# Rounding of packed counts in two instructions, and visit tables in uint16, in a four-layer graph network

## The reference, cut to what matters

```python
h = relu(layernorm(x)); x = x + GIN(h, src, dst)           # segment sum of h[src] by dst, two linear layers
h = relu(layernorm(x)); x = x + Attention(h, edges, ...)   # segment softmax by target, then a linear layer
h = relu(layernorm(x)); x = x + SAGE(h, src, dst)          # mean of h[src] by dst, two linear layers
h = relu(layernorm(x)); x = x + Weighted(h, src, dst, w)   # segment sum of w * h[src], one linear layer
```

## Time and profile before

| | |
|---|---|
| median of 3 runs | 5038.48 us (5023.93, 5038.48, 5147.51) |
| span of the profiled execution | 5145.3 us |
| DVE busy | 3822.7 us (74%) |
| PE busy | 3841.6 us (75%) |
| count layer of layer 0, first to last rounding (L1360) | 1380.7 to 1778.5 us |
| count layer of layer 2, first to last rounding (L1360) | 4184.5 to 4585.7 us |
| granted TensorE clock, mean | 0.909 |

### The profile page before, as it was taken

One profiled execution on the slowest core, in us unless ns is written; L12 is line 12 of the kernel. 1 busy time (PEld: TensorE's weight loads), 2 busy tenths in 40 slices (PEclk: granted clock), 3 DMA queues, 4 the chain that ended last, 5 costly groups with the idle time before them and its releaser, 6 DMA issues. The chain is left out here.

```text
span 5145.3 us, 93266 instructions
## 1 busy us (share of the span) xinstructions
PE 3841.6 (75%) x26234; PEld 2720.9 (53%) x26235; DVE 3822.7 (74%) x6359; ACT 1550.3 (30%) x3023; POOL 2737.6 (53%) x2300
## 2 busy tenths in 40 slices
PE   4685555550199968888888888888886348889999
PEld 2443222220189835555555555555554248888888
DVE  3516999991299989999999999999996699970000
ACT  2372234560101130122333444445552430020000
POOL 3430199996732227777777777777776232210000
PEclk8799999995599989999999999999997569999999
DMA  9674423346155444454555666666665535568887
GB/s 168 175 234 111 97 100 126 159 175 198 66 193 209 163 140 106 120 146 142 157 165 169 184 184 188 193 196 197 205 204 159 186 113 200 200 213 300 298 297 254
DMA packets 594376, 912.02 MB, mean 177 GB/s; under 512 B 107452, under 2 KB 519442, under 8 KB 575022
## 3 DMA queue, kind: packets, MB, share of 16 engines
q1 hardware_dynamic: 413024, 521.23, 31.2%
q10 hardware_dynamic: 117359, 250.68, 13.4%
q0 software_dynamic: 63872, 138.75, 11.3%
HBM read 608.33 MB, written 311.94 MB: 179 GB/s over the span
## 5 line engine op out<-in xcount | busy, mean ns | idle before, releaser
L1964 POOL DMA_INDIRECT at_qg<-q_d,at_slot x1616 | 1601.2, 991 | 495.8 <-issue 492.2
L986 PE MATMUL bw_ps<-bw_mov,bw_sta 128*128 128x392 bf16 x7056 | 1590.0, 349 | 19.2 <-issue 7.2
L986 PEld LDWEIGHTS bw_ps<-bw_mov,bw_sta 128*128 128x128 bf16 x7056 | 640.4, 102 | 365.0 <-issue 95.6
L2007 PE MATMUL at_psk<-at_kp,at_hot 128*128 x4848 | 611.7, 234 | 286.8 <-DVE at_qg L2085 244.4
L1051 POOL DMA_INDIRECT tv_rows<-ed_d,tv_place x101 | 628.2, 6219 | 339.1 <-DMA edv_d<-tv_rows 211.0
L2007 PEld LDWEIGHTS at_psk<-at_kp,at_hot 128*128 128x128 bf16 x4848 | 439.1, 101 | 624.1 <-issue 418.1
L889 PE MATMUL ba_ps<-ba_mov,ba_sta 128*128 128x392 bf16 x1968 | 380.4, 338 | 352.6 <-DVE ba_sta L830 309.1
L874 DVE TENSOR_SCALAR ba_mov<-iota,key,scale 128x392 bf16<-128x392 f16 x1968 | 592.4, 365 | 2.8 <-PEq L853 2.8
L970 DVE TENSOR_TENSOR bw_sta<-bw_raw,kw 128x1024 bf16<-128x1024 bf16 x882 | 561.2, 689 | 0.0
L830 DVE TENSOR_TENSOR bw_mov<-bw_ps,lo 128x3136 bf16<-128x3136 f16 x294 | 523.4, 1780 | 7.6 <-PE bw_ps L986 5.4
L1566 PE MATMUL at_p3t<-tile,room 128*128 128x256 f32 (+1 forms) x2450 | 524.2, 376 | 4.6 <-ACT room L1150 4.6
(11 more groups left out here) (537 smaller groups left out, 4668.3 us busy)
## 6 DMA issues: line engine op xcount, KB each, us to landing
tile<-adw_d SPq DMA_DIRECT2D x23, 6272.0 KB, 18.7
adw_d<-xall ACTq DMA_DIRECT2D x65, 1568.0 KB
adj_d<-ba_stage ACTq DMA_DIRECT2D x50, 1568.0 KB, 5.1
l0raw<-adj_d SPq DMA_DIRECT2D x50, 1568.0 KB, 6.6
tile<-adj_d SPq DMA_DIRECT2D x50, 1568.0 KB, 6.5
adw_d<-bw_stage ACTq DMA_DIRECT2D x33, 1568.0 KB
at_rel<-rel_d SPq DMA_DIRECT2D x101, 512.0 KB
et_attr<-in_edge_attr SPq DMA_DIRECT2D x48, 1024.0 KB
```

The source lines that it names most:

```text
L986: ins = pe.matmul(self.ps[:, bass.DynSlice(place, WCOL)], self.sta[:, k, u // 2, :, u % 2], self.mov[:, u // 2, :, u % 2], start=False, st ...
L1964: pool.indirect_dma_start(out=qg[:, ring, b, :], out_offset=None, in_=q_d[:, :], in_offset=bass.IndirectOffsetOnAxis(ap=slot[:, ring, b:b ...
L2007: ins = pe.matmul(ps_k[:, at:at + KW], hot[:, par, sum(ROUNDS[:r]) + u, :], kp[:].rearrange("p j k n -> p (j k n)")[:, bass.DynSlice(place ...
```

## The change

The rounding of a packed row becomes two instructions: one over the first 48 of the 49 rows of 64 words, and one over the last. The semaphore is raised by the second alone. The four visit tables and their copies in SBUF become uint16; DVE gets one more small conversion for each pair of tables (`firstv_u`). Everything else stands as it was.

```diff
@@ CountLayer.unpack (both count layers)
-        q.odd.inc(ve.tensor_scalar(cast[:, :, HALF:P], raw, ROUND, -ROUND, ALU.add, ALU.add))
+        ve.tensor_scalar(cast[:, 0:NB - 1, HALF:P], raw[:, 0:NB - 1, :], ROUND, -ROUND, ALU.add, ALU.add)
+        q.odd.inc(ve.tensor_scalar(cast[:, NB - 1, HALF:P], raw[:, NB - 1, :], ROUND, -ROUND, ALU.add, ALU.add))
@@ WindowTables
-        self.wt, self.wti, self.cti, self.reg = t("wt", self.groups), t("wti", self.groups, I32), t("cti", self.groups, I32), t("reg", self.groups, I32)
+        self.wt, self.wti, self.cti, self.reg = t("wt", self.groups), t("wti", self.groups, I32), t("cti", self.groups, I32), t("reg", self.groups, U16)
@@ visits_of
-            chain(ve.tensor_copy(w.low[:], w.low_i[:]), ve.tensor_copy(w.high[:], w.high_i[:]))
+            chain(ve.tensor_copy(w.low[:], w.low_i[:]), ve.tensor_copy(w.high[:], w.high_i[:]), ve.tensor_copy(w.firstv_u[:], w.firstv_i[:]))
@@ store_visits
-                S.dma(pool.dma_start(first_d.rearrange("(c q) -> q c", q=P), w.firstv_i[:]))
+                S.dma(pool.dma_start(first_d.rearrange("(c q) -> q c", q=P), w.firstv_u[:]))
@@ build_counts
-        c.wreg, c.vend = ctx.enter_context(nc.sbuf_tensor("ba_wreg", [1, NVISV], I32)), ctx.enter_context(nc.sbuf_tensor("ba_vend", [1, NWV // 2], I32))
+        c.wreg, c.vend = ctx.enter_context(nc.sbuf_tensor("ba_wreg", [1, NVISV], U16)), ctx.enter_context(nc.sbuf_tensor("ba_vend", [1, NWV // 2], U16))
@@ edge_scores
-        c.wreg, c.vend = tables[0:1, :], tables[32:33, 0:NW]
+        c.wreg, c.vend = tables[0:1, 0:NVIS // 2].bitcast(U16), tables[32:33, 0:NW // 2].bitcast(U16)
@@ program
-        c.reg_d = nc.dram_tensor("reg_d", (VG * P,), I32, kind="Internal").ap()
+        c.reg_d = nc.dram_tensor("reg_d", (VG * P,), U16, kind="Internal").ap()
...
```

More of the change, by code:

```diff
@@ L12 @@
 BF16 = mybir.dt.bfloat16
-I16, I32 = mybir.dt.int16, mybir.dt.int32
+I16, I32, U16 = mybir.dt.int16, mybir.dt.int32, mybir.dt.uint16
 ALU = mybir.AluOpType
@@ L118, in __init__ @@
         self.firsts, self.missing, self.base = t("firsts", P), t("missing", self.columns), t("base", blocks)
-        self.firstv, self.firstv_i, self.low, self.high, self.low_i, self.high_i = (t(n, self.columns, dt) for n, dt in (("firstv", F32), ("firstv_i", I32), ("low", F32), ("high", F32), ("low_i", I32), ("high_i", I32)))
+        self.firstv, self.firstv_u, self.firstv_i, self.low, self.high, self.low_i, self.high_i = (t(n, self.columns, dt) for n, dt in (("firstv", F32), ("firstv_u", U16), ("firstv_i", I32), ("low", F32), ("high", F32), ("low_i", I32), ("high_i", I32)))
         self.where, self.under = (t(n, self.columns * self.groups, BF16) for n in ("where", "under"))
-        self.wt, self.wti, self.cti, self.reg = t("wt", self.groups), t("wti", self.groups, I32), t("cti", self.groups, I32), t("reg", self.groups, I32)
+        self.wt, self.wti, self.cti, self.reg = t("wt", self.groups), t("wti", self.groups, I32), t("cti", self.groups, I32), t("reg", self.groups, U16)
 def index_loads(nc, c, src, dst, edge_weight, sb):
@@ L2776, in program @@
         c.edv_d = nc.dram_tensor("edv_d", (NG2, P, 2 * P), F32, kind="Internal").ap()
-        c.reg_d = nc.dram_tensor("reg_d", (VG * P,), I32, kind="Internal").ap()
-        c.first_d = nc.dram_tensor("first_d", (-(-NW // P) * P,), I32, kind="Internal").ap()
-        c.regv_d = nc.dram_tensor("regv_d", (VGV * P,), I32, kind="Internal").ap()
-        c.firstv_d = nc.dram_tensor("firstv_d", (-(-NWV // P) * P,), I32, kind="Internal").ap()
+        c.reg_d = nc.dram_tensor("reg_d", (VG * P,), U16, kind="Internal").ap()
+        c.first_d = nc.dram_tensor("first_d", (-(-NW // P) * P,), U16, kind="Internal").ap()
+        c.regv_d = nc.dram_tensor("regv_d", (VGV * P,), U16, kind="Internal").ap()
+        c.firstv_d = nc.dram_tensor("firstv_d", (-(-NWV // P) * P,), U16, kind="Internal").ap()
         c.rel_d = nc.dram_tensor("rel_d", (NV2, P), F16, kind="Internal").ap()
```

## The result

| | before | changed |
|---|---|---|
| median of the runs | 5031.2 us (5014.4 to 5147.51, 4 runs) | 5375.3 us (5374.39 to 5380.27, 4 runs) |
| span of the profiled execution | 5145.3 us | 5373.2 us |

The ratio is 1.0705, with a 95% interval from 1.0673 to 1.0738: the changed kernel is 7% slower. The one long execution of before, 5147.51 us, is left out of the ratio, so it is a little above 5375.3 / 5031.2. The forecast was 4971 us, within 4940 to 5052, so it is wrong in sign and in size.

A forecast was written before the change was run, and what follows sets the result against it. DVE was taken to bound the count layers, with PE close behind and next to bind. Layer 0's 26 us and layer 2's 41 us make 67, tables zero: 5038.5 - 67 = 4971 us, range 4940 to 5052.

The forecast's parts named there:

- The rounding: Count layers, DVE: 48 rows run at the fast rate, 1.76 us plus about 0.2 for the last row, against 3.41.
- POOL and the turns: Count layers: with POOL standing aside, turns of 7.05 us in layer 0 and 7.10 in layer 2, gaining 67 us.
- PE is the only bound: Rival, count layers: POOL's work fits fully into DVE's idle time; 79 us gained, 4959 us; chance 0.22.
- Exclusion: Count layers: fast DVE instructions and POOL's exclude each other, taking 0.19 to 0.30 us a turn if nothing overlaps.
- the least turn: Count layers: POOL's 1.88 us, the subtraction's 3.42 and the rounding's 1.88 cannot overlap, so at least 7.18 us a turn.
- The tables in uint16: Sequencer table loads in count build and attention: changed load times taken as zero, with 11 us kept either way.
- The number of register loads stays the same: PE's sequencer: still 246 and 294 loads, of some 0.6 and 0.76 us.
- a price on shorter loads: Rival on the uint16 tables: shorter loads bring 11 us and more beyond the 79 us gain, under 4945; chance 0.03.
- DVE has no gaps and PE waits for it, so shorter or longer loads are hidden: Count build, while the first table is read: a changed load time costs or gains nothing.
- a tenth reached the path: Attention stage: if loads changed by half and a tenth reached the path, 294 x 0.38 x 0.1 = 11 us.
- The same mix of executions: Whole kernel: DVE's work beside POOL's gather L1051 is unaltered, so long and short executions should occur as before.
- my sum: Whole kernel: 67 us from the count layers and zero from the tables, so 5038.5 - 67 = 4971 us; chance 0.45.

The follow-up runs named there:

- m1: The control with the split rounding: two rounding instructions, int32 tables, one extra register operation per loaded number; 5028.45 us, ratio 0.996 to the kernel before.
- m0: The control: kernel before (one rounding instruction, int32 tables) with one more register operation on each loaded window number and end; 5109.3 us, ratio 1.0129.
- a4: Changed kernel with ScalarE's end tables back at int32, one register operation more per eviction, PE's window tables still uint16; 5358.09 us, ratio 1.0621 to before.
- o1: Kernel before with split rounding, int32 tables, and TensorE waiting for clear banks twice per octet, not once per visit; 5002.98 us, ratio 0.9823.

## Why the prediction was wrong

**The rounding: right.** 1.75 and 0.19 us were measured for 1.76 and 0.19. An output in fp32r does not keep the fast rate away.

**POOL and the turns: right in the main, a little too careful.** I took 7.05 and 7.10 us a turn, 67 us in all. The changed kernel has 6.97 and 6.86, and gains 81 us in the two layers; m1 against its control gives 80.9 in the median. That is the rival "PE is the only bound", at 79. GpSimd does stand aside: its median for the row masks, 1233 ns in layer 0 in the earlier trace rows, is 4413 and 2529 in the two layers of the changed kernel, and its L1392 has 2945 ns in layer 2, where the same line (L1391) had 464 before. Nothing waits for it. Exclusion was the term of this part that I mis-sized, 12 us for about nothing.

```profile
L1386 POOL TENSOR_SCALAR l0cl_rows<-iota,l0cl_at,row_scale x50: 1232/4413/5592, 1522.0 to 1875.0; 128x256 f32<-128x256 f16 x50
L1386 POOL TENSOR_SCALAR at_cl_rows<-iota,at_cl_at,row_scale x50: 1217/2529/5766, 4467.4 to 4820.6; 128x256 f32<-128x256 f16 x50
```

The 7.18 us that the prediction works out as the least turn, by the rule of the Trainium skill ("SBUF — State Buffer", section "Who interferes with whom"), did not hold: 6.97 and 6.86 were measured, and the measurement decides. The timeline of layer 2 has one place where the two engines overlap, as far as GpSimd's spans can be trusted. L1386 ran on for 1.0 us beside the subtraction, which took 3.58 us in place of 3.42:

```profile
4655.77 2.62 POOL L1386 TENSOR_SCALAR at_cl_rows<-iota,at_cl_at,row_scale 128x256 f32<-128x256 f16 x1 [0.21 <-POOL at_cl_at L1383]
...
4657.40 3.58 DVE L1363 TENSOR_TENSOR cast<-tile,cast 128x3136 fp32r<-128x3136 f32 x1
```

**"The tables in uint16": this step failed, twice.** "The number of register loads stays the same" is true, but I let a load grow by half at most and put a price on shorter loads only among the rivals. It grew to 3.2 times in the count build and 2.7 times in the attention's. A load of another type than the rows show was an operation that the trace of before does not hold, and I had no reason to bound it so tightly. The second failure is "DVE has no gaps and PE waits for it, so shorter or longer loads are hidden". That PE waits for DVE says that DVE is the bound, not by how much. m0 shows how thin the cover was: eight small register operations more lengthened the quiet turn by 0.38 us. The load's 1.33 us more lengthened it by 1.11. Over the 236 octets outside the gates, some of them with a shorter turn early in the build, that is about 250 of the +317 us, and the gates' 60 are the rest. By the same reading "a tenth reached the path" in the attention was off: 294 times 1.33 us are 391 us, and the stretch grew by 219, of which a4 gives 17 to ScalarE's loads. That is still half.

**"The same mix of executions": wrong, and in the changed kernel's favour.** With TensorE's sequencer as the bound VectorE pauses, all gathers get through early, and the long executions are gone: the changed kernel's times lie within 6 us. This gave back part of the loss, 196 us in the profiled pair, whose execution of before was a long one, and some 80 by the medians, if the other stretches are as long there.

**The rest.** The split without the tables, which is what my sum described, gave 81 us in m1 against its control, for the 67 that I forecast; the control itself stands 63 us above before's short executions. Freed of most of that in o1 it is at 0.9823 of the kernel before, where my 4971 is 0.987 of the median, but o1 also waits less often than before does. For the split the forecast holds in the main; for the change it does not.

What stays open is why a narrow load costs more, and why its 1.33 us lengthened the turn by 1.11 and not by all of it. The runs give 74 ns for each number of an eight-word int32 load and 240 for each of uint16. They do not tell whether the sequencer or the path to SBUF makes the difference.

## What to carry to other kernels

A table that a sequencer loads into registers should be int32 even where its numbers are small; if it must be stored narrow, load it as words and split them with register operations. Before a change of type is costed at nothing, look for a row of the same operation in the new type, and if there is none, bound it by factors, not by halves. An engine that waits for another has slack only as long as its sequencer's work is shorter than the turn, and this work is not in its busy time: add up loads and register operations per turn before calling them hidden. And when one stage's pace changes, ask what other engines now run beside it: here GpSimd's gates moved under the build, and the stretch behind it shrank for the same reason.
